# Message pass of a graph network kernel: totals loaded ahead of the masks, caps taken by DVE from the totals, the gate product on GpSimd, row copies by ScalarE and DVE by turns, stores issued by SyncE

## The chip, the cores and the metric

The kernel runs on one core of a Trainium2 chip, as one launch. The metric is the device time in microseconds, the median of several runs. Five engines run their own instruction streams and meet through semaphores: PE (TensorE, matmul), DVE (VectorE), ACT (ScalarE), POOL (GpSimd) and SP (SyncE, which here only issues transfers).

## The reference

Four graph layers run one after the other on 6250 nodes and 200000 edges, sorted by target node, with 64 channels. The change is in the third, a gated convolution:

```python
total = jnp.concatenate([atom_fea[dst], atom_fea[src], edge_fea], axis=1)
total = _batchnorm(total @ fc_w.T + fc_b, bn1_w, bn1_b)      # 128 columns per edge
gate, core = jnp.split(total, 2, axis=1)
messages = jax.nn.sigmoid(gate) * jax.nn.softplus(core)      # 64 columns per edge
aggr = jax.ops.segment_sum(messages, dst, num_segments=N)
```

## The kernel before

The kernel goes through the edges in seven passes. Two of them belong to this layer: `STAT` computes the sums `total @ fc_w.T` before the batch norm, stores them in DRAM (`total_d`) and gathers their mean and variance; `MSG`, the pass that is changed, reads them back and makes the messages and their running sums.

In `MSG` the edges stand in 196 blocks (`NB`). A block holds 512 edges (`BLK`) of each of two halves of the edge list, with 64 channels of each half on the 128 partitions, so that it is a tile of 128 x 1024: 512 columns of gate sums and 512 of core sums. Blocks go in fours (`U`), one round of a hardware loop (`IT` = 49 rounds); `i` counts rounds and `u` the block in a round, and every buffer of the pass but the masks, `pm` and `res` (two of each) stands four times. Every engine has its own code, and all wait through `Ring` semaphores: `s_x.done(engine, p, i, u, back=k)` waits until the producer of `s_x` is done with the block that is `k` before `u`. The code of each engine is written out in order, and this sets the order of the work; nothing is scheduled.

One block passes through these steps:

- SP loads `total_d` into `totals` (`attr_load`, L404, 512 KB; the tile is part of `feat`) once block u - 4 has been scaled (`s_col`), and for every second block a small mask (`mask_load`, L455), for which it waits until the scan three blocks back is over (`s_res`).
- POOL applies the batch norm with two `tensor_scalar` of 512 columns (`affine`, L624), with a scale `bnsc` and a shift `bnbi` per partition, into `zbuf`. The scale and shift of the gate are negated in advance, so that exp of it is exp(-gate).
- DVE caps all 1024 columns at 80 into `ebuf` (`capped`, L1387).
- ACT takes exp and then ln(1 + x) of the 1024 columns (`logs`, L1094 and L1096), and from the gate half exp(-x), the sigmoid, into `zbuf` (`gate`, L1100).
- DVE takes the larger of core and logarithm, the softplus, into `msg` (`softplus`, L1392), multiplies it with the sigmoid (L1485) and runs the segmented running sum (`scan`, L1376), whose mask PE has spread into PSUM (`spread_mask`, L816).
- PE turns the sums back into rows of edges (`turn_back`, L791), ACT copies them out of PSUM into `obuf` (`rows_out`, L1071) and issues their store (L1077, 256 KB) from its own queue, behind a wait for its copy.

The tiles `zbuf` and `ebuf` are parts of `arena`, `msg` and `res` are parts of `work`, `pm` and `pt` of `pn`. In its step for block k DVE does the softplus of k + 1, the cap of k + 2 and the scan of k; ACT does the gate of k + 1, the logs of k + 2 and the rows of k - 1.

Of the kernel before, what the change touches and what calls it, by code (L numbers as in the profile page):

```python
# [18 lines left out]
P = 128  # L19
# [3 lines left out]
J = 4  # L23
# [69 lines left out]
def gnn_kernel(nc, x, src, dst, ea128, ea16, ea64, W0, b0, W1, b1, W2, b2, fcw, fcb, bn1w, bn1b,  # L93
# [15 lines left out]
    with ctx:  # L109
# [80 lines left out]
        bnsc, bnbi = sb("bnsc", [P, 2]), sb("bnbi", [P, 2])  # L190
# [42 lines left out]
        s_col = ring("s_col", {**one(GATHER), MSG: 2})  # L233
# [99 lines left out]
        def _(sp):  # L333
# [66 lines left out]
            def attr_load(p, i, u):  # L400
                b = blk(i, u)
                if p == MSG:
                    s_col.done(sp, p, i, u, back=U)
                    sp.dma_start(totals[:, u, :], total_d[bass.ds(b, 1), :, :].rearrange("a p n -> (a p) n")).then_inc(s_att.sems[u], 16)  # L404
                if p not in (SOFT, STAT, *PNA):
                    return
                if p == SOFT:
                    s_col.done(sp, p, i, u, back=2)
                else:
                    s_eT.done(sp, p, i, u, back=U if p in PNA else 2)  # L410
                if p != MSG:
                    sp.sem_inc(s_in_order, 1)
                for h, e0 in ((0, 0), (1, BASE1)):
                    rows = bass.ds(b * BLK + e0, BLK)
                    if p == SOFT:
                        to = attr[:, u % 2, 0:2 * J * F].rearrange("p (j h c) -> p j h c", j=J, h=2)[:, :, h, :]
                        of = ea64[rows, :].rearrange("(p j) c -> p j c", j=J)
                    elif p == STAT:
                        to = attr[:, u % 2, h * J * P:(h + 1) * J * P]
                        of = ea128[rows, :].rearrange("(p j) c -> p (j c)", j=J)  # L420
                    elif p in PNA:
                        to = attr_to[u][:, h * F:h * F + F]
                        of = ea16[rows, :].rearrange("(p j) c -> p (j c)", j=J)
                    sp.dma_start(to, of).then_inc(s_att.sems[u], 16)
# [17 lines left out]
            def mask_load(p, i, u):  # L442
# [14 lines left out]
                for h in range(2):  # L457
                    sp.dma_start(keep[h * F:h * F + F, u // 2, :],
                                 keep_d[h:h + 1, bass.ds(blk(i, u) * BLK, 2 * BLK)].broadcast_to([F, 2 * BLK]))\
                      .then_inc(s_kee.sems[u], 16)  # L460

# [41 lines left out]
            for p in range(7):  # L503
# [15 lines left out]
                if p not in GCN:  # L519
# [25 lines left out]

                if p in READS:
# [27 lines left out]
        def _(g):  # L574
# [44 lines left out]
            def affine(i, u):  # L619
# [23 lines left out]
            for p in range(7):  # L643
# [4 lines left out]
                if p == MSG:  # L648
                    g.wait_ge(s_wc, 3)
                    for u in range(U):  # L650
                        affine(0, u)
                    with g.Fori(1, IT) as i:
                        for u in range(U):
                            affine(i, u)
                else:
# [36 lines left out]
        def _(pe):  # L692
# [82 lines left out]
            def turn_back(p, i, u):  # L775
# [11 lines left out]
                s_rev.done(pe, p, i, u, back=1)  # L787
                for k in range(UNITS[p]):
                    of = top[:, u, :] if p == SOFT and k == 0 else res[:, u % 2, k, :]
                    for j in range(J):  # L790
                        last = nc.tensor.transpose(pt[:, k, j * P:(j + 1) * P], of[:, 1 + j:1 + BLK:J], ident[:, :])  # L791
# [255 lines left out]
        def _(act):  # L1047
# [12 lines left out]

            def rows_out(p, i, u):
# [4 lines left out]
                to = rows_to[u] if K == 3 else obuf_f[:, u * BLK:(u + 1) * BLK]  # L1066
# [9 lines left out]
                r = runs3_d if K == 3 else runs1_d  # L1076
                act.dma_start(r.rearrange("(h n) c -> h n c", h=2)[:, bass.ds(blk(i, u) * BLK, BLK), :]  # L1077
# [33 lines left out]
            def body(p, i, end):  # L1111
                for u in range(U):
# [20 lines left out]
                    if p == MSG:  # L1133
# [82 lines left out]
            for p in range(7):  # L1216
# [23 lines left out]
                if p == MSG:  # L1240
                    rows_out(p, IT - 1, U - 1)
# [38 lines left out]
        def _(dve):  # L1280
# [103 lines left out]
            def capped(i, u):  # L1384

                s_col.done(dve, MSG, i, u)
                TS(ebuf[:, u, :], zbuf[:, u, :], CAP, None, ALU.min).then_inc(s_arg.sems[u], 1)  # L1387

            def softplus(i, u):
# [43 lines left out]
            def step(p, i, u, end):  # L1433
# [60 lines left out]
            def edge_pass(p):  # L1494
# [18 lines left out]
                for u in range(U):  # L1513
                    step(p, IT - 1, u, True)

# [360 lines left out]
            link(TS(bnbi[:, 0:1], bnbi[:, 0:1], -1.0, None, ALU.mult))  # L1876
            dve.sem_inc(s_wc, 1)
# [111 lines left out]
```

## Time and profile before

| | us |
|---|---|
| median of 3 runs | 10983.7 (10974.28 to 10992.69) |
| the profiled execution | 10998.39 |
| its span | 10996.7 |
| `MSG` within it, first cap to last row copy | 5731.3 to 6561.8 |

Outside `MSG` nothing is touched. Most of the time of the kernel is in the passes that gather node rows by indirect transfers on POOL; POOL is busy 64% of the span, PE 58%, DVE 52% and ACT 29%. `MSG` is the stretch of 830 us in slices 21 to 23 of the page's 40, in which ACT and DVE are busiest. The columns of the views are told with the rows below.

### The profile page before, as it was taken

The page shows a single profiled execution, that of the slowest core. Times are in us where ns is not written, and L with a number is a line of the kernel's source. Part 1 is how long each engine was busy: PE and PEld are TensorE (multiplying, and loading weights), DVE is VectorE, ACT ScalarE, POOL GpSimd, SP SyncE. Part 2 cuts the span into 40 slices and gives each one's busy share as a digit, 9 for nine tenths or more (in the row PEclk, how much of TensorE's full clock was granted, in tenths as well). Part 3 has the DMA queues.
Part 4 walks back from the last instruction along what each step waited for, and adds up shares of the span by engine and source line. Part 5 has one row for each costly group of instructions (what it writes and reads, how often), then busy time and mean ns, then how long its engine had stood idle before and what let it go on. Part 6 is the DMA issues. An engine that isn't in the chain of part 4 may idle for free. (4 is left out here: it accounts for less than half of the span.)

```text
span 10996.7 us, 138229 instructions
## 1 busy us (share of the span) xinstructions
PE 6379.7 (58%) x42657; PEld 5452.4 (50%) x42755; DVE 5713.8 (52%) x8038; ACT 3161.8 (29%) x4908; POOL 6995.6 (64%) x6971
## 2 busy tenths in 40 slices
PE   3666666548888566666653333455555455555553
PEld 2555555437788555445431113454544445555453
DVE  3555555689951655555557764333333443333335
ACT  1333333227710011111117761222222222222221
POOL 4777777715500577777764444777777767777774
PEclk9888888769999888888875556777777777777776
DMA  7666666514457477777765542444444334444442
GB/s 126 188 195 192 195 190 193 162 67 183 194 193 279 149 234 235 237 239 233 235 198 187 187 162 66 126 122 126 124 126 122 103 102 124 124 124 124 126 122 72
DMA packets 1299105, 1783.39 MB, mean 162 GB/s; under 512 B 619145, under 2 KB 794044, under 8 KB 1289322
## 3 DMA queue, kind: packets, MB, share of 16 engines
q1 hardware_dynamic: 816519, 882.68, 24.9%
q10 hardware_dynamic: 269696, 616.64, 15.2%
q0 software_dynamic: 212704, 281.43, 11.4%
q8 instruction: 136, 2.23, 0.1%
q14 instruction: 50, 0.41, 0.0%
HBM read 922.11 MB, written 857.87 MB: 162 GB/s over the span
## 5 line engine op out<-in xcount | busy, mean ns | idle before, releaser
L615 POOL DMA_INDIRECT arena<-table_d,idx_src x3136 | 2963.6, 945 | 1121.5 <-issue 955.3
L759 PE MATMUL pn<-work,wblk 128*128 128x128 f32 x3136 | 959.3, 405 | 1887.7 <-DMA arena<-table_d,idx_src 1887.7
L615 POOL DMA_INDIRECT arena<-in_x_dram,idx_src x1568 | 1523.7, 972 | 591.4 <-issue 477.0
L615 POOL DMA_INDIRECT arena<-tsrc_d,idx_src x1568 | 1482.1, 945 | 478.0 <-issue 478.0
L1329 DVE TENSOR_SCALAR idx_src<-src_all 128x8 int32 (+1 forms) x784 | 139.5, 179 | 3124.0 <-PE pn L760 2392.9
L759 PEld LDWEIGHTS pn<-work,wblk 128*128 128x128 f32 x3136 | 755.2, 296 | 1963.5 <-DMA arena<-table_d,idx_src 1005.9
L760 PE MATMUL pn<-ident,arena 128*128 128x128 f32 x4704 | 1292.6, 371 | 0.0
L1071 ACT ACTIVATE arena<-pn 128x512 f32<-128x512 f32 x1470 | 793.0, 594 | 1274.1 <-PE pn L791 1167.1
L760 PEld LDWEIGHTS pn<-ident,arena 128*128 128x128 f32 x4704 | 1096.6, 286 | 0.0
L749 PE MATMUL pn<-work,weT 128*128 128x512 f32 x784 | 553.9, 796 | 663.7 <-DMA arena<-tsrc_d,idx_src 635.8
L1376 DVE TENSOR_TENSOR_SCAN work<-keep,work,pn 128x512 f32<-128x512 bf16 x588 | 752.7, 1280 | 274.4 <-PE ph L772 203.0
L757 PE MATMUL pn<-ident,attr 128*128 128x128 f32 x1568 | 422.6, 362 | 627.8 <-DMA arena<-in_x_dram,idx_src 621.6
L791 PE MATMUL pn<-ident,work 128*128 128x128 f32 x2352 | 440.5, 334 | 510.7 <-ACT obuf L1071 499.6
L1087 ACT ACTIVATE work<-pe_ 128x1024 f32<-128x1024 f32 x196 | 200.9, 1025 | 1785.9 <-PE pe_ L730 1785.9
L757 PEld LDWEIGHTS pn<-ident,attr 128*128 128x128 f32 x1568 | 327.5, 258 | 741.3 <-issue 613.1
L624 POOL TENSOR_SCALAR arena<-feat,bnsc,bnbi 128x512 f32<-128x512 f32 x392 | 373.9, 966 | 486.7 <-DMA feat<-total_d 486.7
L791 PEld LDWEIGHTS pn<-ident,work 128*128 128x128 f32 x2352 | 351.0, 213 | 607.2 <-issue 315.7
L751 PEld LDWEIGHTS pn<-ident,arena 128*128 128x128 f32 x3136 | 509.5, 230 | 265.9 <-issue 265.9
L784 PE MATMUL pn<-ident,work 128*128 128x128 f32 x3528 | 582.6, 314 | 3.8 <-DVE work L1376 3.8
L640 POOL DMA_INDIRECT arena<-near_d,dlo x37 | 356.3, 9630 | 330.5 <-PE pe_ L900 276.2
L784 PEld LDWEIGHTS pn<-ident,work 128*128 128x128 f32 x3528 | 553.5, 215 | 4.2 <-DVE work L1376 4.2
L1179 ACT ACTIVATE feat<-pn 128x784 bf16<-128x784 f32 x592 | 487.2, 825 | 153.9 <-PE pn L911 144.6
(364 smaller groups left out, 13511.0 us busy)
## 6 DMA issues: line engine op xcount, KB each, us to landing
runs_d<-arena ACTq DMA_DIRECT2D x588, 768.0 KB
adj_d<-feat SPq DMA_DIRECT2D x37, 3136.0 KB, 10.7
feat<-adj_d SPq DMA_DIRECT2D x37, 3136.0 KB, 10.9
seed_d<-nothing SPq DMA_DIRECT2D x392, 256.0 KB
arena<-seed_d SPq DMA_DIRECT2D x392, 256.0 KB, 6.8
attr<-in_edge_attr_dram SPq DMA_DIRECT2D x392, 256.0 KB
feat<-total_d SPq DMA_DIRECT2D x196, 512.0 KB
keep<-keep_d SPq DMA_DIRECT2D x588, 128.0 KB
```

Source lines behind the costliest of these rows:

```text
L615: g.indirect_dma_start(out=to, out_offset=None, in_=table, in_offset=bass.IndirectOffsetOnAxis(ap=idx, axis=0))\
L624: g.tensor_scalar(zbuf[:, u, part * BLK:(part + 1) * BLK], totals[:, u, part * BLK:(part + 1) * BLK], bnsc[:, part:part + 1], bnbi[:, part ...
L749: mm(to, weT[:, :], eT[:, s, h * BLK:(h + 1) * BLK], start=True, stop=False, skip_group_check=True)
L751: last = mm(to[:, j:BLK:J], gat[:, u, j, h, :], ident[:, :], start=False, stop=True, skip_group_check=True)
L757: mm(to, attr[:, u % 2, j * P:(j + 1) * P], ident[:, :], start=True, stop=False, skip_group_check=True)
L759: mm(to, wblk[:, PNA.index(p), j, :], feat_to[u], start=True, stop=False, skip_group_check=True)
L760: last = mm(to, gat1[:, u, j * P:(j + 1) * P], ident[:, :], start=(p in (GCN1, GCN2)), stop=True, skip_group_check=True)
L784: last = nc.tensor.transpose(row_bank(u, k)[:, j * P:(j + 1) * P], res[:, u % 2, k, 1 + j:1 + BLK:J], ident[:, :])
L791: last = nc.tensor.transpose(pt[:, k, j * P:(j + 1) * P], of[:, 1 + j:1 + BLK:J], ident[:, :])
L1071: last = A(to.rearrange("p (h j k c) -> p k j h c", h=2, j=J, k=K)[:, k, :, :, :], of.rearrange("p (j h c) -> p j h c", j=J, h=2), ACT.Copy)
L1179: A(adj[:, m % 2, :, g * GROUP:(g + 1) * GROUP].rearrange("p k (b n) -> p k b n", b=2), pn[:, 2 * (k % 2):2 * (k % 2) + 2, 0:4 * KC].rearr ...
L1376: return SCAN(res[:, s, k, 1:BLK + 1], mask, data, res[:, 1 - s, k, BLK:BLK + 1], ALU.mult if mul else ALU.add, ALU.add if mul else ALU.mi ...
```

## The change

- SP issues the loads of two blocks ahead of their mask, where the mask came between them (`attr_load` of u and u + 1, then `mask_load` of u). A load now also waits for the cap of block u - 4 (`s_arg`), since DVE reads `totals` too.
- The cap no longer goes through POOL's `zbuf`. DVE computes min(total x scale, 80 - shift) for each half, two instructions of 512 columns, where `room` = 80 - shift is made once, and ACT adds the shift inside exp, which becomes two instructions of 512 columns with a bias per partition.
- POOL scales only the core half (one instruction a block) and takes over the product of softplus and sigmoid (`gated`), which stands in its queue behind the scaling of the next block.
- The row copy is ACT's for blocks 0 and 2 of a round and DVE's for blocks 1 and 3 (`gated_rows` on either). PE turns rows into two PSUM banks by turns where one was used.
- The stores of the pass are issued by SP (`gated_store`): block 0 of the round before behind the loads and the mask of blocks 0 and 1, blocks 1 to 3 of it behind those of 2 and 3.

```diff
@@ SP: attr_load @@
                     s_col.done(sp, p, i, u, back=U)
+                    sp.sem_inc(s_in_order, 1)
+                    s_arg.done(sp, p, i, u, back=U)
...
+            def gated_store(i, u):
+                s_rev.done(sp, MSG, i, u)
+                sp.sem_inc(s_in_order, 1)
+                sp.dma_start(runs1_d...[:, bass.ds(blk(i, u) * BLK, BLK), :]..., obuf_f[:, u * BLK:(u + 1) * BLK]...)
...
                             if p == MSG:
-                                attr_load(p, i, u)
-                                mask_load(p, i, u)
+                                if u % 2 == 0:
+                                    attr_load(p, i, u)
+                                    attr_load(p, i, u + 1)
+                                    mask_load(p, i, u)
+                                for v in ((0,), (), (1, 2, 3), ())[u]:
+                                    gated_store(i - 1, v)
@@ POOL: affine @@
-                for part in range(2):
-                    g.tensor_scalar(zbuf[:, u, part * BLK:(part + 1) * BLK], totals[:, u, part * BLK:(part + 1) * BLK],
-                                    bnsc[:, part:part + 1], bnbi[:, part:part + 1], ALU.mult, ALU.add).then_inc(s_col.sems[u], 1)
+                g.tensor_scalar(zbuf[:, u, BLK:], totals[:, u, BLK:], bnsc[:, 1:2], bnbi[:, 1:2], ALU.mult, ALU.add)\
+                 .then_inc(s_col.sems[u], 1)
+            def gated(i, u):
+                s_sg.done(g, MSG, i, u)
+                s_top.done(g, MSG, i, u)
+                g.sem_inc(s_go, 1)
+                g.tensor_tensor(msg[:, u, :], msg[:, u, :], zbuf[:, u, 0:BLK], ALU.mult).then_inc(s_cus.sems[u], 1)
...
                         for u in range(U):
                             affine(i, u)
+                            gated(i - 1 if u == 0 else i, (u - 1) % U)
@@ PE: turn_back @@
-                s_rev.done(pe, p, i, u, back=1)
+                s_rev.done(pe, p, i, u, back=2 if p == MSG else 1)
@@ ACT: gated_rows, logs, body @@
+                A(obuf_f[:, u * BLK:(u + 1) * BLK]..., pt[:, u % 2, :]..., ACT.Copy).then_inc(s_rev.sems[u], 1)
...
-                A(ebuf[:, u, :], ebuf[:, u, :], ACT.Exp).then_inc(s_exp.sems[u], 1)
+                A(ebuf[:, u, 0:BLK], ebuf[:, u, 0:BLK], ACT.Exp, bias=bnbi[:, 0:1])
+                A(ebuf[:, u, BLK:], ebuf[:, u, BLK:], ACT.Exp, bias=bnbi[:, 1:2]).then_inc(s_exp.sems[u], 1)
...
-                        if u > 0:
-                            rows_out(p, i, u - 1)
-                        elif not (isinstance(i, int) and i == 0):
-                            rows_out(p, i - 1, U - 1)
+                        if u % 2:
+                            gated_rows(i, u - 1)
@@ DVE: capped, gated_rows, softplus, step @@
-                s_col.done(dve, MSG, i, u)
-                TS(ebuf[:, u, :], zbuf[:, u, :], CAP, None, ALU.min).then_inc(s_arg.sems[u], 1)
+                s_att.done(dve, MSG, i, u)
+                s_sg.done(dve, MSG, i, u, back=U)
+                s_top.done(dve, MSG, i, u, back=U)
+                TS(ebuf[:, u, 0:BLK], totals[:, u, 0:BLK], bnsc[:, 0:1], room[:, 0:1], ALU.mult, ALU.min)
+                TS(ebuf[:, u, BLK:], totals[:, u, BLK:], bnsc[:, 1:2], room[:, 1:2], ALU.mult, ALU.min).then_inc(s_arg.sems[u], 1)
+                V.tensor_copy(obuf_f[:, u * BLK:(u + 1) * BLK]..., pt[:, u % 2, :]...).then_inc(s_rev.sems[u], 1)
...
+                s_col.done(dve, MSG, i, u)
                 s_ln.done(dve, MSG, i, u)
+                s_res.done(dve, MSG, i, u, back=U)
                 TT(msg[:, u, :], zbuf[:, u, BLK:], ebuf[:, u, BLK:], ALU.max).then_inc(s_top.sems[u], 1)
...
-                    s_sg.done(dve, p, i, u)
-                    s_top.done(dve, p, i, u)
-                    TT(msg[:, u, :], msg[:, u, :], zbuf[:, u, 0:BLK], ALU.mult).then_inc(s_cus.sems[u], 1)
...
+                    if u == 2:
+                        gated_rows(i, 1)
+                    if u == 0 and not (isinstance(i, int) and i == 0):
+                        gated_rows(i - 1, U - 1)
@@ DVE: before the pass @@
+            link(TS(room[:, :], bnbi[:, :], -1.0, CAP, ALU.mult, ALU.add))
```

DVE's queue in the hardware loop, blocks 0 and 1 of a round, before. L1485 is the product, L1392 the softplus of the next block, L1387 the cap of the one after, L1376 the scan:

```order
L1485 TENSOR_TENSOR work<-work,arena 128x512
L1392 TENSOR_TENSOR work<-arena 128x512
L78 ISA
L1387 TENSOR_SCALAR arena<-arena 128x1024
L78 REGISTER_ALU
L1376 SCALAR_TENSOR_TENSOR work<-pn,work 128x512
L1485 TENSOR_TENSOR work<-work,arena 128x512
L1392 TENSOR_TENSOR work<-arena 128x512
L1387 TENSOR_SCALAR arena<-arena 128x1024
L1376 SCALAR_TENSOR_TENSOR work<-pn,work 128x512
```

The same place now, with the lines of the changed file: L1435 is the softplus, L1420 and L1421 the cap, L1427 the row copy, L1407 the scan:

```order
L1435 TENSOR_TENSOR work<-arena 128x512
L78 ISA
L1420 TENSOR_SCALAR arena<-feat,bnsc,room 128x512
L1421 TENSOR_SCALAR arena<-feat,bnsc,room 128x512
L78 ISA
L1427 COPY obuf<-pn 128x4x2x64
L78 REGISTER_ALU
L1407 SCALAR_TENSOR_TENSOR work<-pn,work 128x512
L1435 TENSOR_TENSOR work<-arena 128x512
L1420 TENSOR_SCALAR arena<-feat,bnsc,room 128x512
L1421 TENSOR_SCALAR arena<-feat,bnsc,room 128x512
L1407 SCALAR_TENSOR_TENSOR work<-pn,work 128x512
```

The product has left DVE's queue, the cap is two instructions on `feat` (the totals) with scalars per partition, and a copy stands ahead of the scan in every second step.

ACT's queue in the loop, two steps before. L1100 is the gate, L1094 and L1096 exp and ln, L1071 the row copy, L1077 its store:

```order
L1100 ACTIVATE arena<-arena 128x512
L1094 ACTIVATE arena<-arena 128x1024
L1096 ACTIVATE arena<-arena 128x1024
L78 ISA
L1071 ACTIVATE obuf<-pn 128x4x2x64
L1077 ISA
L1077 DMA runs_d<-obuf 128x2x256
```

Two steps of it now, with L1135 the gate, L1128 and L1129 exp, L1131 ln and L1093 the row copy:

```order
L1135 ACTIVATE arena<-arena 128x512
L78 REGISTER_ALU
L1128 ACTIVATE arena<-arena,bnbi 128x512
L1129 ACTIVATE arena<-arena,bnbi 128x512
L1131 ACTIVATE arena<-arena 128x1024
L1135 ACTIVATE arena<-arena 128x512
L1128 ACTIVATE arena<-arena,bnbi 128x512
L1129 ACTIVATE arena<-arena,bnbi 128x512
L1131 ACTIVATE arena<-arena 128x1024
L78 ISA
L1093 ACTIVATE obuf<-pn 128x4x2x64
```

The store has left the queue, and the copy stands in every second step.

## Rows read from the trace of the kernel before

**Rows 1.** The page: span and instruction count.

```profile
span 10996.7 us, 138229 instructions
```

**Rows 2.** Groups by form, 5725 to 6575 us: count | busy us, mean ns | idle before, releaser.

```profile
L624 POOL TENSOR_SCALAR arena<-feat,bnsc,bnbi 128x512 f32<-128x512 f32 x392 | 373.9, 966 | 486.7 <-DMA feat<-total_d 486.7
L1376 DVE TENSOR_TENSOR_SCAN work<-pn,work 128x512 f32<-128x512 f32 x196 | 249.8, 1274 | 0.0
L1096 ACT ACTIVATE arena<-arena 128x1024 f32<-128x1024 f32 x196 | 207.1, 1057 | 6.2
...
L1392 DVE TENSOR_TENSOR work<-arena 128x512 f32<-128x512 f32 x196 | 149.7, 764 | 73.3 <-ACT arena L1096 67.1
L1485 DVE TENSOR_TENSOR work<-work,arena 128x512 f32<-128x512 f32 x196 | 142.9, 729 | 23.4 <-DVE work L1376 9.9
...
L1387 DVE TENSOR_SCALAR arena<-arena 128x1024 f32<-128x1024 f32 x196 | 135.5, 691 | 84.9 <-POOL arena L624 84.9
L1100 ACT ACTIVATE arena<-arena 128x512 f32<-128x512 f32 x196 | 123.5, 630 | 136.5 <-ACT obuf L1071 136.4
```

**Rows 3.** Line L1094 (exp): ns min/median/max, first and last start, its waits.

```profile
L1094 ACT ACTIVATE arena<-arena x196: 1038/1056/1057, 5732.0 to 6553.5; 128x1024 f32<-128x1024 f32 x196
its engine sat idle before it (us, times) until:
  DVE arena L1387: 88.0, 87
```

**Rows 4.** Timeline, 6000 to 6018: start, duration, engine, line [idle before, releaser].

```profile
6001.83 0.69 DVE L1392 TENSOR_TENSOR work<-arena 128x512 f32<-128x512 f32 x1 [0.48 <-ACT arena L1096]
6001.95 4.00 POOL L624 TENSOR_SCALAR arena<-feat,bnsc,bnbi 128x512 f32<-128x512 f32 x4 [4.57 <-DMA feat<-total_d]
...
6003.95 0.69 DVE L1387 TENSOR_SCALAR arena<-arena 128x1024 f32<-128x1024 f32 x1 [1.43 <-POOL arena L624]
...
6004.68 1.06 ACT L1094 ACTIVATE arena<-arena 128x1024 f32<-128x1024 f32 x1 [1.10 <-DVE arena L1387]
...
6006.45 1.20 SPq L404 DMA_DIRECT2D feat<-total_d  x2
...
6008.28 0.63 ACT L1100 ACTIVATE arena<-arena 128x512 f32<-128x512 f32 x1 [0.97 <-ACT obuf L1071]
...
6008.82 1.04 ACT L1094 ACTIVATE arena<-arena 128x1024 f32<-128x1024 f32 x1
...
6009.89 1.06 ACT L1096 ACTIVATE arena<-arena 128x1024 f32<-128x1024 f32 x1
6010.01 1.52 POOL L624 TENSOR_SCALAR arena<-feat,bnsc,bnbi 128x512 f32<-128x512 f32 x2 [4.06 <-DMA feat<-total_d]
6010.85 0.58 ACT L1071 ACTIVATE obuf<-pn 128x512 f32<-128x512 f32 x1
6010.98 1.10 DVE L1392 TENSOR_TENSOR work<-arena 128x512 f32<-128x512 f32 x1 [0.85 <-ACT arena L1096]
...
6012.00 0.68 DVE L1387 TENSOR_SCALAR arena<-arena 128x1024 f32<-128x1024 f32 x1
6012.05 0.63 ACT L1100 ACTIVATE arena<-arena 128x512 f32<-128x512 f32 x1 [0.61 <-ACT obuf L1071]
...
6012.71 1.06 ACT L1094 ACTIVATE arena<-arena 128x1024 f32<-128x1024 f32 x1
```

**Rows 5.** The transfer queues, 5725 to 6575 us: packets, MB, share of 16 engines.

```profile
q1 hardware_dynamic: 28760, 103.21, 36.7%
q10 hardware_dynamic: 53312, 51.39, 17.2%
```

**Rows 6.** Single lines: ns min/median/max; two with a scalar per partition (L1523, L1828).

```profile
L1523 DVE TENSOR_SCALAR arena<-arena,valid x6: 254/254/254, 6636.3 to 10937.0; 128x64 f32<-128x64 f32 x6
L1567 DVE TENSOR_SCALAR nrow<-nrow x3: 195/195/195, 6649.9 to 10942.3; 128x64 f32<-128x64 f32 x3
L1828 DVE TENSOR_SCALAR arena<-dlo x698: 278/286/289, 3059.9 to 3629.4; 128x128 f32<-128x128 f32 x175
L1755 DVE COPY feat<-pn x13: 279/682/692, 3660.4 to 3702.5; 128x512 f32<-128x512 f32 x12, 128x128 f32<-128x128 f32 x1
L624 POOL TENSOR_SCALAR arena<-feat,bnsc,bnbi x392: 766/773/1717, 5729.7 to 6551.5; 128x512 f32<-128x512 f32 x196
```

**Rows 7.** Timeline, 5737.1 to 5738.3 us, DVE and POOL at once.

```profile
5736.91 0.69 DVE L1392 TENSOR_TENSOR work<-arena 128x512 f32<-128x512 f32 x1 [0.49 <-ACT arena L1096]
5737.05 1.72 POOL L624 TENSOR_SCALAR arena<-feat,bnsc,bnbi 128x512 f32<-128x512 f32 x1
5737.53 0.68 DVE L1387 TENSOR_SCALAR arena<-arena 128x1024 f32<-128x1024 f32 x1
5738.13 1.27 DVE L1376 TENSOR_TENSOR_SCAN work<-pn,work 128x512 f32<-128x512 f32 x1
```

More of the change, by code:

```diff
@@ L189, in gnn_kernel @@
         agg2 = sb("agg2", [P, 2])
-        bnsc, bnbi = sb("bnsc", [P, 2]), sb("bnbi", [P, 2])
+        bnsc, bnbi, room = sb("bnsc", [P, 2]), sb("bnbi", [P, 2]), sb("room", [P, 2])
         nrow = sb("nrow", [P, 4, F])
@@ L232, in gnn_kernel @@
         s_eC = ring("s_eC", one((STAT, *PNA)))
-        s_col = ring("s_col", {**one(GATHER), MSG: 2})
+        s_col = ring("s_col", {**one(GATHER), MSG: 1})
         s_zero_out = sem("s_zero_out")
@@ L460, in mask_load @@
                       .then_inc(s_kee.sems[u], 16)
+            def gated_store(i, u):
+                s_rev.done(sp, MSG, i, u)
+                sp.sem_inc(s_in_order, 1)
+                sp.dma_start(runs1_d.rearrange("(h n) c -> h n c", h=2)[:, bass.ds(blk(i, u) * BLK, BLK), :]
+                             .rearrange("h (p j) c -> p h (j c)", j=J),
+                             obuf_f[:, u * BLK:(u + 1) * BLK].rearrange("p (h q) -> p h q", h=2)).then_inc(s_out.sems[u], 16)
             def adjacency_moves(p):
@@ L544, in _ @@
                     continue
+                if p == MSG:
+                    for u in range(U):
+                        gated_store(IT - 1, u)
                 if p in READS:
@@ L651, in _ @@
                         affine(0, u)
+                    for u in range(U - 1):
+                        gated(0, u)
                     with g.Fori(1, IT) as i:
@@ L654, in _ @@
                             affine(i, u)
+                            gated(i - 1 if u == 0 else i, (u - 1) % U)
+                    gated(IT - 1, U - 1)
                 else:
@@ L790, in turn_back @@
                     for j in range(J):
-                        last = nc.tensor.transpose(pt[:, k, j * P:(j + 1) * P], of[:, 1 + j:1 + BLK:J], ident[:, :])
+                        last = nc.tensor.transpose(pt[:, u % 2 if p == MSG else k, j * P:(j + 1) * P], of[:, 1 + j:1 + BLK:J], ident[:, :])
                 last.then_inc(s_row.sems[u], 1)
@@ L1059, in masks, with gated_rows @@
                 A(neg[:, v, :], keep[:, v, :], ACT.Copy, scale=BIG, bias=-BIG).then_inc(s_neg.sems[u], 1)
+            def gated_rows(i, u):
+                s_row.done(act, MSG, i, u)
+                s_out.done(act, MSG, i, u, back=U)
+                A(obuf_f[:, u * BLK:(u + 1) * BLK].rearrange("p (h j c) -> p j h c", h=2, j=J),
+                  pt[:, u % 2, :].rearrange("p (j h c) -> p j h c", j=J, h=2), ACT.Copy).then_inc(s_rev.sems[u], 1)
             def rows_out(p, i, u):
@@ L1065, in rows_out @@
                 K = UNITS[p]
-                to = rows_to[u] if K == 3 else obuf_f[:, u * BLK:(u + 1) * BLK]
+                to = rows_to[u]
                 for k in range(K):
@@ L1075, in rows_out @@
                 s_rev.done(act, p, i, u)
-                r = runs3_d if K == 3 else runs1_d
-                act.dma_start(r.rearrange("(h n) c -> h n c", h=2)[:, bass.ds(blk(i, u) * BLK, BLK), :]
+                act.dma_start(runs3_d.rearrange("(h n) c -> h n c", h=2)[:, bass.ds(blk(i, u) * BLK, BLK), :]
                               .rearrange("h (p j) c -> p h (j c)", j=J),
@@ L1239, in _ @@
                 body(p, IT - 1, True)
-                if p == MSG:
-                    rows_out(p, IT - 1, U - 1)
                 if p == SOFT:
@@ L1384, in capped, with gated_rows, softplus @@
             def capped(i, u):
+                s_att.done(dve, MSG, i, u)
[3 more added lines that the diff above has]
+                TS(ebuf[:, u, BLK:], totals[:, u, BLK:], bnsc[:, 1:2], room[:, 1:2], ALU.mult, ALU.min).then_inc(s_arg.sems[u], 1)
+            def gated_rows(i, u):
+                s_row.done(dve, MSG, i, u)
+                s_out.done(dve, MSG, i, u, back=U)
+                V.tensor_copy(obuf_f[:, u * BLK:(u + 1) * BLK].rearrange("p (h j c) -> p j h c", h=2, j=J),
+                              pt[:, u % 2, :].rearrange("p (j h c) -> p j h c", j=J, h=2)).then_inc(s_rev.sems[u], 1)
+            def softplus(i, u):
                 s_col.done(dve, MSG, i, u)
-                TS(ebuf[:, u, :], zbuf[:, u, :], CAP, None, ALU.min).then_inc(s_arg.sems[u], 1)
-            def softplus(i, u):
                 s_ln.done(dve, MSG, i, u)
+                s_res.done(dve, MSG, i, u, back=U)
                 TT(msg[:, u, :], zbuf[:, u, BLK:], ebuf[:, u, BLK:], ALU.max).then_inc(s_top.sems[u], 1)
@@ L1514, in edge_pass @@
                     step(p, IT - 1, u, True)
+                if p == MSG:
+                    gated_rows(IT - 1, U - 1)
             over_f = lambda a: a.unsqueeze(2).broadcast_to([P, a.shape[1], F])
```

## The prediction

> **What bounds the kernel now.** The change touches only `MSG`, so I first read the groups of its stretch [rows 2]. Every engine has idle time: POOL is busy 374 of some 830 us, the three DVE instruction kinds and the scan sum to 678, ACT's groups shown to 536 with the row copies to come. No engine is full, so the time is set by a circle of waits or by arrivals. The pace is one block in (6553.5 - 5732.0) / 195 = 4.21 us [rows 3].
>
> The timeline shows the circle [rows 4]. ln of a block begins at 6009.89 and ends at 6010.95; the softplus starts 0.03 later; the cap of the next block follows at 6012.00 and ends at 6012.68; exp starts at 6012.71. Then exp and ln again. Softplus (block k + 1), cap (k + 2), exp and ln (k + 2), softplus (k + 2): each waits for the one before, whatever the engines have free. With the softplus at its usual pitch of 0.61 (0.69 less the 0.08 by which back-to-back DVE instructions overlap), the circle is 0.03 + 0.61 + 0.69 + 0.03 + 1.04 + 0.03 + 1.06 = 3.49 us.
>
> Three things lift it to 4.21. First, ACT has a circle of its own: from one exp to the next in these rows exp takes 1.07 to the start of ln, 0.96 until the row copy starts, 1.20 until the gate starts (the copy, a wait for it and the issue of its store), and 0.54 from gate to exp [rows 4]: 3.77 us. The page has 136.5 us of idle time before the gate behind the copy, 0.70 a block [rows 2]. Second, loads come late: at 6001.83 the softplus is done in good time, but POOL gets its block only at 6001.95, the cap waits 1.43 us for it and exp another 1.10 behind [rows 4]. The cap waited 84.9 us for POOL, exp 88.0 for the cap, of which 27.1 lie before the first block: 61, or 0.31 a block [rows 2, 3]. Third, DVE and POOL get in each other's way: the softplus takes 0.764 on average against 0.69 undisturbed, POOL's scaling 0.966 against 0.773 [rows 2, 6], and the softplus of 1.10 us started while POOL was in its second instruction [rows 4]. 3.77 plus 0.31 plus 0.1 or so is the 4.2 seen.
>
> **The change, part by part.** I work out the new circle and then look whether anything else is longer.
>
> *ACT.* Exp becomes two instructions of 512. One of 512 lasts 0.63 [rows 2], and a next one that waits for nothing starts 0.54 after it (gate at 8.28, exp at 8.82) [rows 4]. So 0.54 + 0.63 = 1.17 in place of 1.04: +0.13. ln stays 1.06, and waits 0.03 for exp. ACT's own circle loses the store and the wait for the copy, and every second copy: gate 0.54, exp 0.54 + 0.66, ln 1.06, half a copy 0.25, in all 3.05 us. It stops being a bound; between the end of ln and the next exp it has at most copy and gate, 1.0 us, beside the 1.5 that DVE needs there.
>
> *DVE, the cap.* Two instructions of 512 with scalars per partition. One with such a scalar takes 254 ns for 64 columns, against 195 without: +59 ns; from 64 to 128 columns it adds 32 ns, the same 0.5 ns a column as without [rows 6]. So the cap's pace per column (1024 in 691 ns) is kept: 0.286 + 384 x 0.52 ns = 0.486 us for 512 [rows 2, 6]. Its pitch is 0.06 less, 0.42, by the overlap of DVE's neighbours. The pair lasts 0.42 + 0.49 = 0.91 in place of 0.69: +0.22. No row has two such scalars; another 59 ns on each would make it 1.03, and a half of the old cap each 0.76. I take 0.91.
>
> *DVE, waits.* The softplus now stands behind the scan and five waits. Those on blocks long finished come after the one on ln, so I take 0.10 from ln to the softplus in place of 0.03.
>
> *New circle:* 0.10 + 0.61 + 0.91 + 0.04 + 1.17 + 0.03 + 1.06 = 3.92 us. With the low ends of lag and cap 3.70, with the high cap 4.04.
>
> *DVE's load.* Softplus 0.61, cap 0.84, scan 1.2, and in every second step a copy out of PSUM, 0.68 by the copy of the same size in L1755, pitch 0.6 [rows 6]: 3.3 us in such a step, plus 0.35 for waits that can only be passed when the scan is over. 3.7 is just under 3.92, so the copy is covered by DVE's wait for ln; if the cover goes, a step with a copy costs what is over.
>
> *The product on POOL.* It needs softplus and sigmoid, and the scan needs it a whole step later, some 4 us, so its duration is hidden unless it is over 3 us. No row shows POOL with two inputs; the nearest is its scaling at 0.77 [rows 6], which bounds it from below, and twice that, 1.54, from above. POOL is then busy 0.8 + 0.8 to 1.5 of 3.9 us. I take 1.2. The Trainium skill (GPSIMD Engine Reference, "Elementwise — side-by-side cycle accounting") gives 4497 ns for an addition of 2048 columns on GpSimd, 1.96 times DVE's; a quarter is 1.1 us, an estimate from that page which no row here shows.
>
> *Loads.* The cap of block u needed POOL's scaling, two instructions; now it needs only the load, 1.5 us earlier. In the order of SP's queue the loads of blocks 0 and 1 stand behind the last store of the round before, which waits for DVE's row copy at 2.3 us into the step of block 0, four blocks ahead; the cap that needs it comes two steps and 0.7 us after that step began, 8.5. One load takes from its issue at 6006.45 to POOL at 6010.01 3.56 us, with a store beside it [rows 4]; a store occupies the 16 engines for 0.172 x 850 / 196 = 0.75 us and a load for 1.6 [rows 5]. Load behind a store: 2.6 + 3.6 + 0.8 = 7.0, 1.5 us early. Loads of 2 and 3 have more. So the 0.31 a block goes. All of it now stands in one queue, which has to be busy 2.35 of 3.92 us.
>
> *Ends of the pass.* The first cap comes 1.6 us earlier (two scalings of POOL), `room` costs 0.2. PE's second bank takes nothing off the circle: PE waits in it anyway.
>
> **The sum.** 195 x (4.21 - 3.92) = 57, plus 1.4, say 58 us less. The profiled execution lasts 10998.4 (span 10996.7 [rows 1]), 14.7 over the median of 10983.7, so I give the change against either: 10940 profiled, median 10926. Range of the mechanism itself: 3.70 gives -100, 4.04 gives -35.
>
> **Rivals.**
>
> *Loads stay late* (a queue with stores ahead of loads). For it: SP now waits for ACT and DVE copies before it may load, and any lag of these is passed on. Against: the 1.5 us reckoned above. Price: the 0.31 of before comes back on top of 3.92: 4.23, time as before, 10983, "no change".
>
> *POOL's product blocks the cap* (the slower side). The product becomes ready when softplus and sigmoid are, that is while DVE starts the first half of the cap. If POOL gets to memory between the two halves, the second waits for the whole product, and the circle with it: 1.2 - 0.15 = 1.05 us. In every second step (after odd blocks ACT copies first, so the product comes too late to hurt) that gives 3.92 + 0.52 = 4.44: +45, 11029; in every step 4.97: +148, 11132. It decides from 0.3 us a block on. For it: DVE instructions are held when POOL is in one, softplus 1.10 in place of 0.69 [rows 4]. Against: at 5737.05 a scaling of POOL was pending, DVE went from softplus to cap without a gap, and POOL lasted 1.72, until 0.56 after the cap's end [rows 7]; so it is DVE's neighbour that gets in first. One case, but the one wanted. Besides, POOL has two waits and a semaphore to pass before the product.
> The Trainium skill (SBUF — State Buffer, "Who interferes with whom") says that DVE instructions with two inputs in SBUF or in the two-port mode, and those of GpSimd, take the shared port for their whole duration, and the other blocks fully. The trace agrees: 1.10 and 1.72 are about a whole instruction of the other more, less 0.15 to 0.3. Its rule speaks against this change, which gives POOL an instruction of two inputs and DVE two short ones in place of one.
>
> *DVE becomes the bound.* If copies and waits make 4.1 in the steps with a copy, the mean is 4.0: -40, 10943; it lies in the range.
>
> **How the numbers follow.** The circle at 3.92, with DVE's share in it: 0.78. Loads late: 0.10. POOL blocks the cap: 0.12, a third of it so mild (under 0.3 us a block) that the result is no slower. What can be told from no change here is 0.2%, 22 us. Faster: 0.78 and a few of each rival, 0.82. Same: 0.09. Slower: 0.09. Range: from 3.75 (-90) to the lower end of the rivals, 10980.
>
> **What would show it.** Exp first to last start over 195 at 3.85 to 4.0 us; no wait of the cap for a load; the gate no longer behind a row copy for 136 us; cap halves near 0.49; the softplus waiting for ln in every step; POOL's product 0.8 to 1.5. Wrong if the cap's second half averages over 0.8 (blocked by POOL), if DVE waits for `total_d`, or if the scan waits for POOL.

## The result

| | before, us | this kernel, us | ratio, 95% interval |
|---|---|---|---|
| changed kernel | 10982.83 | 11116.45 (11108.69 to 11139.15) | 1.0128 (1.0113 to 1.0143) |

Slower by 134 us, where 58 less was forecast; the time lies 136 us over the upper end of the range. It is the second rival (GpSimd's product blocks DVE's cap, 11029 to 11132), which had 0.12. The prediction's own sign for it, a second half of the cap over 0.8 us on average, is there: 1.26.

The groups of the message pass in the profile after, 5700 to 6720 us; they answer to [rows 2]. L1420 and L1421 are the two halves of the cap, L1128 and L1129 exp, L1131 ln, L1135 the gate, L1435 the softplus, L649 the product:

```profile
L649 POOL TENSOR_TENSOR work<-work,arena 128x512 f32<-128x512 f32 x196 | 273.8, 1397 | 492.4 <-ACT arena L1135 274.7 <-DVE work L1435 217.7
L1407 DVE TENSOR_TENSOR_SCAN work<-pn,work 128x512 f32<-128x512 f32 x196 | 249.2, 1271 | 0.1
L1421 DVE TENSOR_SCALAR arena<-feat,bnsc,room 128x512 f32<-128x512 f32 x196 | 246.0, 1255 | 0.0
...
L641 POOL TENSOR_SCALAR arena<-feat,bnsc,bnbi 128x512 f32<-128x512 f32 x196 | 168.0, 857 | 71.7 <-DMA feat<-total_d 71.6
...
L1128 ACT ACTIVATE arena<-arena,bnbi 128x512 f32<-128x512 f32 x196 | 141.4, 722 | 349.5 <-DVE arena L1421 349.5
L1129 ACT ACTIVATE arena<-arena,bnbi 128x512 f32<-128x512 f32 x196 | 138.3, 706 | 0.0
...
L1420 DVE TENSOR_SCALAR arena<-feat,bnsc,room 128x512 f32<-128x512 f32 x196 | 106.0, 541 | 4.2 <-DMA feat<-total_d 4.2
```

The two halves of the cap are the same instruction on different columns, yet the first takes 0.54 us and the second 1.26 on average. The single line of each shows the first and last start of exp, which give the pace as in [rows 3]:

```profile
L1128 ACT ACTIVATE arena<-arena,bnbi x196: 706/722/724, 5717.9 to 6675.4; 128x512 f32<-128x512 f32 x196
L1421 DVE TENSOR_SCALAR arena<-feat,bnsc,room x196: 538/1485/1515, 5717.4 to 6673.8; 128x512 f32<-128x512 f32 x196
```

(6675.4 - 5717.9) / 195 = 4.91 us a block, 0.70 more than before; times 195 that is 136 us, the whole of the loss. The timeline of one step, with its releasers, answers to [rows 4]:

```profile
6200.25 0.63 ACT L1135 ACTIVATE arena<-arena 128x512 f32<-128x512 f32 x1
6200.45 0.69 DVE L1435 TENSOR_TENSOR work<-arena 128x512 f32<-128x512 f32 x1 [0.89 <-ACT arena L1131]
...
6201.06 0.54 DVE L1420 TENSOR_SCALAR arena<-feat,bnsc,room 128x512 f32<-128x512 f32 x1
6201.31 1.41 POOL L649 TENSOR_TENSOR work<-work,arena 128x512 f32<-128x512 f32 x1 [1.67 <-DVE work L1435]
6201.51 1.49 DVE L1421 TENSOR_SCALAR arena<-feat,bnsc,room 128x512 f32<-128x512 f32 x1
6202.92 1.27 DVE L1407 TENSOR_TENSOR_SCAN work<-pn,work 128x512 f32<-128x512 f32 x1
6203.03 0.72 ACT L1128 ACTIVATE arena<-arena,bnbi 128x512 f32<-128x512 f32 x1 [2.15 <-DVE arena L1421]
...
6214.70 1.06 ACT L1131 ACTIVATE arena<-arena 128x1024 f32<-128x1024 f32 x1
...
6215.79 0.69 DVE L1435 TENSOR_TENSOR work<-arena 128x512 f32<-128x512 f32 x1 [1.30 <-ACT arena L1131]
...
6216.85 0.54 DVE L1421 TENSOR_SCALAR arena<-feat,bnsc,room 128x512 f32<-128x512 f32 x1
6216.97 1.55 POOL L649 TENSOR_TENSOR work<-work,arena 128x512 f32<-128x512 f32 x1 [3.03 <-ACT arena L1135]
```

The softplus ends at 6201.14; 0.17 later the product is ready, while the first half of the cap runs. The product goes next, the second half waits for it, and exp behind it. In the last two rows, where ScalarE's row copy made the gate late, the product becomes ready 0.12 after the second half began: that half lasts 0.54, and the product waits. In the other step with a row copy the softplus and the cap are 0.2 late too, and the product still comes 0.03 ahead of the second half. Of the 196 second halves 147 last over 1 us and 49 do not: the first two blocks, and one step of the round in 47 rounds.

### The profile page after: what moved, and what is told of

It is laid out like the page before. It is cut to its first block, busy times and chain, and to the rows that moved or that the text cites. A ratio compares the mean times of both kernels' runs of the same rounds, so it can differ in the third digit from the quotient of the medians.

```text
span 11112.7 us, 139561 instructions
## 1 busy us (share of the span) xinstructions
PE 6432.9 (58%) x42755; PEld 5482.6 (49%) x42755; DVE 5808.1 (52%) x8137; ACT 3165.2 (28%) x5006; POOL 7063.8 (64%) x6971
## 4 chain that ended last, share of the span: by engine, by line
POOL 53%; issue 20%; DVE 11%; PE 5%; ACT 5%; DMA 4%; SPq 1%; POOLq 0%; DVEq 0%; ACTq 0%
POOL arena L633 52%; DVE obuf L1853 2%; DVE arena L1421 2%; ACT arena L1131 2%; DMA feat<-adj_d 2%; POOL feat L714 2%; PE pn L968 1%; PE pn L955 1%; ACT arena L1128 1%; DMA arena<-near_d,dlo 1%; ACT arena L1129 1%; DVE neg L1853 1%; DVE pos L1853 1%; DVE arena L1420 1%; PE ph L955 1%
## 5 line engine op out<-in xcount | busy, mean ns | idle before, releaser
L1407 DVE TENSOR_TENSOR_SCAN work<-keep,work,pn 128x512 f32<-128x512 bf16 x588 | 752.8, 1280 | 276.1 <-PE ph L800 205.8
L1121 ACT ACTIVATE work<-pe_ 128x1024 f32<-128x1024 f32 x196 | 200.7, 1024 | 1783.3 <-PE pe_ L758 1783.3
L649 POOL TENSOR_TENSOR work<-work,arena 128x512 f32<-128x512 f32 x196 | 273.8, 1397 | 492.4 <-ACT arena L1135 274.7
```

The source lines that it names most:

```text
L1407: return SCAN(res[:, s, k, 1:BLK + 1], mask, data, res[:, 1 - s, k, BLK:BLK + 1], ALU.mult if mul else ALU.add, ALU.add if mul else ALU.mi ...
```

## The experiments

"Pace" is exp's first to last start over 195, from the profile of each run; before it is 4.21, after 4.91. Ratios are to the kernel before on the same chip. The third column is the difference of the medians, and the ratio is not exactly their quotient: for `c_load_order` the one gives 58 us and the other 68. `h_half_product`, `u_first_half_two_inputs`, `x_one_input_scalars` and `y_one_input_constants` leave out part of the arithmetic and serve for timing alone. On two of the chips the kernel before takes 13279 and 13380 us, since the other passes take longer (`c_load_order` reaches its first exp at 7279 us in place of 5732); in the message pass, undisturbed instructions last the same on all, so the pace is compared across them and times are not.

| run | pace, us | this - before, us | ratio, 95% interval |
|---|---|---|---|
| `a_product_after_cap` | 4.19 | +17 | 1.0011 (0.9977 to 1.0045) |
| `b_product_on_dve` | 4.18 | +9 | 1.0006 (0.9980 to 1.0031) |
| `h_half_product` | 4.50 | +68 | 1.0037 (1.0007 to 1.0067) |
| `c_load_order` | 3.88 | -58 | 0.9949 (0.9922 to 0.9975) |
| `d_rows_and_stores` | 3.99 | -49 | 0.9955 (0.9938 to 0.9971) |
| `w_rows_third_store_act` | 3.77 | -89 | 0.9940 (0.9921 to 0.9958) |
| `m_cap_first` | 4.11 | -22 | 0.9981 (0.9972 to 0.9991) |
| `n_cap_first_pool_product` | 4.33 | +18 | 1.0016 (1.0006 to 1.0026) |
| `o_after_cap_first` | 3.54 | -141 | 0.9872 (0.9856 to 0.9889) |
| `v_cap_first_third_store_act` | 3.47 | -140 | 0.9904 (0.9881 to 0.9928) |
| `u_first_half_two_inputs` | 5.28 | +168 | 1.0130 (1.0096 to 1.0165) |
| `x_one_input_scalars` | 4.19 | -12 | 0.9988 (0.9977 to 0.9999) |
| `y_one_input_constants` | 4.42 | +28 | 1.0029 (1.0016 to 1.0041) |
| `r_split_exp` | 4.26 | -11 | 1.0001 (0.9983 to 1.0019) |

**Is it the product between the halves?** Three edits of the changed kernel.

```diff
+                s_arg.done(g, MSG, i + (u + 1) // U, (u + 1) % U)     # in gated: wait for the next cap
```

> The changed kernel, but GpSimd's product of block k waits also until DVE has capped block k + 1 (the last block excepted). Theory (the product takes the shared way to memory between the two halves of the cap): the second half falls from 1.49 to 0.54 us in every block, and the pace from 4.91 to the 4.15 that the changed kernel's undisturbed steps show, so 195 x 0.76 = 148 us less than the changed kernel: 10968. Rival (the exp with a bias per partition, the two short instructions or the stores on SyncE's queue cost the time, and the long second half is only where the waiting shows): the pace stays over 4.6 us, 11055 or more.

Measured: the second half at 0.535/0.541/0.544 us, the pace 4.19. The theory holds; the rival (4.6 and more) falls.

```diff
+                    TT(msg[:, u, :], msg[:, u, :], zbuf[:, u, 0:BLK], ALU.mult).then_inc(s_cus.sems[u], 1)   # DVE
-                            gated(i - 1 if u == 0 else i, (u - 1) % U)                                      # POOL
```

> The changed kernel, but DVE does the product, ahead of the softplus, as before; GpSimd has only the scaling of the core half. Theory (blocked cap): the second half lasts 0.54; DVE then has 0.61 + 0.61 + 0.99 + 1.20 + half of 0.60 = 3.7 us a block and 0.35 of waits behind the scan, so the pace is 4.15 to 4.25 us: 10972 to 10991. Rival (exp and stores cost the time): 4.8 to 5 us, 11100 or more.

Measured: pace 4.18, as expected; second half 0.54 in the median. In 28 blocks it lasts 0.83 or more: there GpSimd's scaling of the core half gets in between the halves, of which more below.

```diff
-                g.tensor_tensor(msg[:, u, :], msg[:, u, :], zbuf[:, u, 0:BLK], ALU.mult)...
+                g.tensor_tensor(msg[:, u, 0:BLK // 2], msg[:, u, 0:BLK // 2], zbuf[:, u, 0:BLK // 2], ALU.mult)...
```

> The changed kernel, with GpSimd's product on 256 of its 512 columns only (the rest of the messages stays the softplus without the gate). Theory (the cap's second half waits for the whole of the product): it falls from 1.49 by what the product gets shorter, about 0.6, to 0.9 us, and the pace from 4.91 to about 4.5: 11036. Rival (a collision has a fixed price whatever the length): the second half stays near 1.49 and the time at 11116.

The second half of the cap (L1421) and the product (L649) in this run:

```profile
L1421 DVE TENSOR_SCALAR arena<-feat,bnsc,room x196: 539/946/976, 7302.9 to 8180.5; 128x512 f32<-128x512 f32 x196
L649 POOL TENSOR_TENSOR work<-work,arena x196: 722/850/1012, 7308.3 to 8185.1; 128x256 f32<-128x256 f32 x196
```

The product got shorter by 0.54 (median 1.387 to 0.850), and so did the second half (1.485 to 0.946). The wait follows the length of GpSimd's instruction one to one; the pace of 4.50 is the one expected.

**What the other parts bring.** The load order alone, in the kernel before:

```diff
-                                attr_load(p, i, u)
-                                mask_load(p, i, u)
+                                if u % 2 == 0:
+                                    attr_load(p, i, u)
+                                    attr_load(p, i, u + 1)
+                                    mask_load(p, i, u)
```

> The kernel before, with the loads of two blocks issued ahead of their mask and nothing else. Theory (the loads were late because they stood behind a mask that waits for a scan): the cap's waits for GpSimd behind a load go (0.31 us a block) and the pace falls from 4.21 to 3.9: 10923. Rival (the loads are late because the transfers are slow, or the circle of ScalarE takes over at once): 4.1 to 4.2 us, 10960 to 10983.

The cap waited 5.9 us in all for GpSimd, where [rows 2] has 84.9; pace 3.88. The theory holds. The load order alone brings the 58 us that the prediction gave the whole change (66 by the pace).

`d_rows_and_stores` adds the stores by SyncE, the copies by turns and the two banks, and keeps scaling, cap and product as before:

> The kernel before with the parts of the change that move no arithmetic: loads ahead of masks, stores by SyncE, row copies by ScalarE and DVE by turns, two PSUM banks for the rows. Scaling of both halves (GpSimd), one cap of 1024 columns and the product (DVE) as before. Theory (these parts are the gain, the cap in halves and the product on GpSimd are the loss): circle 0.10 + 0.61 + 0.69 + 0.04 + 1.05 + 0.03 + 1.06 = 3.58 us, DVE's load 3 x 0.61 + 1.20 + 0.30 + 0.35 = 3.7; pace 3.7, the pass 722 us in place of 821, 100 us less than before. Rival (the load order alone is the gain, the rest nothing, as DVE gets the copies): 3.87 as with the load order alone, 60 to 65 us less than before.

Both miss: 3.99 is slower than the load order alone. The timeline shows SyncE, GpSimd and the cap (L1412):

```profile
6007.59 3.14 SPq L467 DMA_DIRECT2D runs_d<-obuf  x3
...
6011.42 1.00 SPq L405 DMA_DIRECT2D feat<-total_d  x2
...
6015.62 3.23 POOL L640 TENSOR_SCALAR arena<-feat,bnsc,bnbi 128x512 f32<-128x512 f32 x3 [5.65 <-DMA feat<-total_d]
...
6017.60 0.69 DVE L1412 TENSOR_SCALAR arena<-arena 128x1024 f32<-128x1024 f32 x1 [1.43 <-POOL arena L640]
```

The loads are issued behind three stores that take 3.1 us to get out, since the third waits for DVE's copy, and the cap then waits for them. Moving only that store to ScalarE:

```diff
-                                for v in ((0,), (), (1, 2, 3), ())[u]:
+                                for v in ((0,), (), (1, 2), ())[u]:
+                        if u == 1 and not (isinstance(i, int) and i == 0):     # ScalarE
+                            gated_store(i - 1, U - 1)
```

> d_rows_and_stores, but the store of block 3 of a round is issued by ScalarE instead of SyncE, so that no load stands behind a wait for DVE's row copy. Theory (in d_rows_and_stores every fourth step lasts 4.66 us in place of 3.77 because the next loads stand behind that store): the long step shrinks by the 1.5 to 2 us that the loads are issued earlier, as far as it was caused by them: pace 3.78 to 3.85 in place of 3.99. Rival (the loads are late because all stores share their queue and go first): 3.95 to 4.0 as before.

3.77: the long step of 4.66 is 3.76. The theory holds, and most of the 100 us that `d_rows_and_stores` should have shown is there (89) once this wait is out of the queue of loads.

**Breaking the circle.** In DVE's step the cap of block k + 2 goes ahead of the softplus of k + 1:

```diff
-                        softplus(i + (u + 1) // U, (u + 1) % U)
-                        capped(i + (u + 2) // U, (u + 2) % U)
+                        capped(i + (u + 2) // U, (u + 2) % U)
+                        softplus(i + (u + 1) // U, (u + 1) % U)
```

> As d_rows_and_stores, and DVE caps block k + 2 before it takes the softplus of block k + 1. Theory (the circle softplus, cap, exp, ln sets the pace): the cap no longer waits for ln, the circle is gone, DVE's load of 3.4 to 3.6 us is the bound: 3.5, 140 us less than before. Rival (DVE was full already): 3.7 as without, 100 less.

> As m_cap_first, with the product on GpSimd (which scales both halves too). Theory (shared way to memory: GpSimd 0.77 + 0.77 + 1.27 less some 0.2 each, DVE 0.69 for the cap and 0.69 for the softplus, one at a time): 3.4 to 3.6 us, no better than m_cap_first. Rival (each engine's own load counts): ScalarE's 3.0 to 3.1 us is the bound, 220 us less than before.

> The changed kernel with one thing other: DVE caps block k + 2 before the softplus of block k + 1. The product needs that softplus, so it can't come between the halves of the cap, and ln is no longer in the circle. Theory: the second half lasts 0.54, ScalarE's load 1.34 + 0.03 + 1.06 + 0.54 + 0.25 = 3.2 us is the bound, with what collisions add 3.3 to 3.4: 160 to 175 us less than before. Rival (another cost of the change, as the exp with bias or the stores on one queue, holds the pace): 4.1 us or more as with the product behind the cap.

The first two miss. `m_cap_first` is slower than `d_rows_and_stores`: it has the same late loads (GpSimd waits 403.8 us for them) and needs them earlier by one softplus; that this is all of the 0.12 us was not tested. In `n_cap_first_pool_product` GpSimd's queue makes a new circle, here softplus (L1429), product (L648), two scalings and the cap (L1416):

```profile
6201.02 0.68 DVE L1429 TENSOR_TENSOR work<-arena 128x512 f32<-128x512 f32 x1
...
6201.89 1.27 POOL L648 TENSOR_TENSOR work<-work,arena 128x512 f32<-128x512 f32 x1 [1.61 <-DVE work L1429]
...
6203.14 1.52 POOL L640 TENSOR_SCALAR arena<-feat,bnsc,bnbi 128x512 f32<-128x512 f32 x2
6204.69 0.69 DVE L1416 TENSOR_SCALAR arena<-arena 128x1024 f32<-128x1024 f32 x1 [1.79 <-POOL arena L640]
6205.30 0.69 DVE L1429 TENSOR_TENSOR work<-arena 128x512 f32<-128x512 f32 x1
```

4.28 us from softplus to softplus, each released by the one before or next behind it in its queue. In `o_after_cap_first` the cap needs no scaling, so this circle is not there: pace 3.54, 141 us less than before and 275 less than the changed kernel (134 more and 141 less than before). It beats both, and its rival of 4.1 us falls; but its theory promised 3.3 to 3.4 us and 160 to 175 less, with a second half of 0.54 throughout. In 48 of 196 blocks that half lasts 0.83 or more, since GpSimd's scaling gets in:

```profile
6103.57 0.55 DVE L1420 TENSOR_SCALAR arena<-feat,bnsc,room 128x512 f32<-128x512 f32 x1 [0.23 <-DVE work L1407]
6103.59 1.01 POOL L641 TENSOR_SCALAR arena<-feat,bnsc,bnbi 128x512 f32<-128x512 f32 x1
...
6104.04 0.84 DVE L1421 TENSOR_SCALAR arena<-feat,bnsc,room 128x512 f32<-128x512 f32 x1
```

That is 0.07 us a block of DVE's time (whether all of it reaches the pace was not tested), and late loads are another 0.07 of the pace, as the next run shows; the rest of the shortfall is open.

`v_cap_first_third_store_act` is that kernel with the edit of the third store:

> o_after_cap_first with the same edit of the third store. Theory: its step of 3.89 falls to 3.5, the pace from 3.54 to 3.45: 18 us less than o_after_cap_first, 155 to 160 less than the kernel before. Rival (the loads share a queue with the stores): the same as o_after_cap_first, 141 less.

Pace 3.47, its step of 3.89 is 3.52. The profile bears the step out, and 14 of the 18 us between the two. The 155 to 160 us less than before are not reached: 140 by the times, 145 by the pace. The times of this run and of `o_after_cap_first`, on different chips, cannot rank the two.

**Why the product gets in, when a scaling in [rows 7] did not.** The first half of the cap as an instruction with two inputs:

```diff
-                TS(ebuf[:, u, 0:BLK], totals[:, u, 0:BLK], bnsc[:, 0:1], room[:, 0:1], ALU.mult, ALU.min)
+                TT(ebuf[:, u, 0:BLK], totals[:, u, 0:BLK], totals[:, u, BLK:], ALU.min)
```

> The changed kernel with the first half of the cap replaced by the smaller of gate and core sums, an instruction with two inputs from memory (0.69 us in place of 0.54; the gate is then not what the reference wants). The question is why GpSimd got in between the two halves here, where a scaling that waited while DVE went from softplus to cap in the kernel before did not. Theory A (a two-input instruction hands on to the next one of DVE, an instruction in the two-port mode does not): the second half lasts 0.54 in most blocks, the product 1.8 to 2.0, and the pace is 4.2 to 4.4 us: about 11010. Theory B (GpSimd gets in whenever it waits at the end of a DVE instruction): the second half lasts 1.3 to 1.5, the pace is 4.9 to 5.1: 11120 or more.

Second half 1.486 in the median, long in 194 of 196 blocks: Theory A falls, since the product gets in behind a DVE instruction of either kind. The pace of 5.28 is over the 4.9 to 5.1 of Theory B, by the longer first half (0.14) and the blocks that are now hit as well. Then GpSimd's, with one input in the product's place:

```diff
-                g.tensor_tensor(msg[:, u, :], msg[:, u, :], zbuf[:, u, 0:BLK], ALU.mult)...
+                g.tensor_scalar(msg[:, u, :], msg[:, u, :], bnsc[:, 1:2], bnbi[:, 1:2], ALU.mult, ALU.add)...   # x
+                g.tensor_scalar(msg[:, u, :], msg[:, u, :], 0.5, 0.25, ALU.mult, ALU.add)...                    # y
```

> The changed kernel with GpSimd's product replaced by a scaling of the softplus, one input and two scalars per partition, in the same place and behind the same waits (the gate is left out of the message). Theory (it is the two-input instruction that gets in): the second half lasts 0.54 in every block, the replacement 1.1 to 1.4 where it waits for it, and the pace is 4.1 to 4.2 us, 0 to 20 us less than the kernel before. Rival (any GpSimd instruction that becomes ready in the first half gets in): the second half lasts about 1.0, the pace is 4.5 us, 55 us more.

> As x_one_input_scalars, with constants in place of the scalars per partition (the gate is left out of the message). Theory (number of inputs): as there, second half 0.54, pace 4.1 to 4.2 us. Rival (a scaling comes late to memory only because it fetches its scalars first): the second half lasts about 1.0 and the pace is 4.5 us.

The second half of the cap in x, and then in y, each with GpSimd's instruction:

```profile
L1421 DVE TENSOR_SCALAR arena<-feat,bnsc,room x196: 537/541/546, 5720.7 to 6537.9; 128x512 f32<-128x512 f32 x196
L649 POOL TENSOR_SCALAR work<-work,bnsc,bnbi x196: 768/1122/1193, 5726.3 to 6542.2; 128x512 f32<-128x512 f32 x196
```

```profile
L1421 DVE TENSOR_SCALAR arena<-feat,bnsc,room x196: 539/839/874, 5724.1 to 6586.3; 128x512 f32<-128x512 f32 x196
L649 POOL TENSOR_SCALAR work<-work x196: 617/738/898, 5729.6 to 6590.8; 128x512 f32<-128x512 f32 x196
```

In x, with scalars per partition, it waits until DVE's second half is over and never delays the cap; in y, with constants and also one input, it gets in between and costs the cap 0.3 us. So my theory of the number of inputs falls, and the rival of y holds in kind (it expected 1.0 and 4.5; measured 0.84 and 4.42): the scalars make the difference.

They do not keep GpSimd out, though; they make it need a longer lead. Over all runs I took the places where a scaling with scalars per partition was pending as the first half of the cap gave way to the second. It got in 124 times, with leads of 0.38 to 1.01 us from its start to that of the second half (in `b_product_on_dve`, `o_after_cap_first` and `v_cap_first_third_store_act`), and 269 times it did not, with leads of 0.35 or less. In x the leads are 0.18 or less. A product or a scaling with constants needs no more than 0.03 and 0.02. From the softplus to a cap, the place of [rows 7] with its lead of 0.48, no scaling got in with a lead under 0.66; over that some did and some did not. What GpSimd does in that lead, and why DVE's instruction matters to a scaling and not to the product, is not shown.

**The price of exp.** In the kernel before, exp in two halves with no bias per partition:

> The kernel before with exp in two instructions of 512 columns and no bias per partition. In the changed kernel each of the two lasts 0.72 and 0.71 where the gate, of the same size, lasts 0.63. Theory (the bias per partition costs 0.09): 0.63 for both here, the pace as before or 0.1 more: 10983 to 11003. Rival (it is the place of the tile or the missing scale): 0.71 here too.

```profile
L1094 ACT ACTIVATE arena<-arena x196: 612/629/632, 7309.7 to 8140.9; 128x512 f32<-128x512 f32 x196
L1095 ACT ACTIVATE arena<-arena x196: 612/613/617, 7310.3 to 8141.5; 128x512 f32<-128x512 f32 x196
```

0.63 and 0.61, against 0.72 and 0.71 with the bias: the bias per partition costs 0.09 each. The time is the same as before within 0.2%, the pace 0.05 longer.

## Why the prediction was wrong

- *POOL blocks the cap.* This is the step that failed. The prediction had the mechanism and its place, gave it 0.12, and turned it down by one row: a scaling that let DVE pass [rows 7]. That row shows an instruction with scalars per partition and a lead of 0.48 us; the product has no such scalars, and `x_one_input_scalars` and `y_one_input_constants` show that without them an instruction gets in at the short leads of this place. The estimate that the product comes too late after odd blocks was wrong as well: it is late enough in one step of four. 147 of 196 blocks by 0.95 us are 0.71 us a block, and 4.19 (with the product held back) + 0.71 = 4.90. That the rival's upper case, 1.05 us in every step on top of 3.92, gives 4.97 beside the measured 4.91 is luck: its circle was 0.27 too short, and its price a block 0.34 too high.
- *The new circle at 3.92.* Mis-sized even without a collision: `a_product_after_cap` gives 4.19, no gain, so this step alone would have sunk the forecast of 58 us less. The pair of exp takes 0.63 + 0.71 = 1.34 in place of 1.17, since the bias was costed at nothing; the pair of the cap 0.45 + 0.54 = 0.99 in place of 0.91. Together 0.25 of the 0.27 missing. For exp a rule would have helped that the prediction did not look up: the Trainium skill (ScalarE: Activation LUTs, "What ACT_TABLE_LOAD costs") gives 0.09 us for each operand per partition, and `r_split_exp` agrees.
- *The product's duration*, 1.2, hidden: it is 1.27 free, and its duration was indeed not what hurt in the scan, which never waits for it; it hurt in the cap. Costing an instruction by who waits for its result left out who waits for the memory.
- *Loads.* Right for the changed kernel: the cap waits 4.2 us in all for them. The reason is that its cap reads the sums itself. In `d_rows_and_stores`, where a scaling stands between, the same queue order costs 0.22 us a block, the first rival in another kernel.
- *The softplus behind five waits*: 0.10 was taken from ln to the softplus. The ln before the softplus of 6215.79 is fast to follow (6214.70 + 1.06 = 6215.76, 0.03 later), the one before 6200.45 ends at 6200.22, 0.23 earlier. In `a_product_after_cap` two steps of a round take 4.09 to 4.10 and two 4.29, with lags of 0.03 and 0.23, so the mean lag is 0.13: the last 0.02 to 0.03 of the 0.27. Why two of the four are late is open.
- *DVE as the bound*: not seen. DVE waits 216 us for ln.
- *The Trainium skill's rule* on the shared port (SBUF — State Buffer, "Who interferes with whom"), cited against the change, was the better guide than the single row: `h_half_product` shows the cap waiting for the product, 0.54 less for 0.54 less. The section also says that the order of issue, and not the kind of instruction, decides who blocks whom. The product agrees (0.03 us ahead of the second half it goes first, 0.11 behind it does not); the scaling of `x_one_input_scalars` does not, if issue is its start in the profile, which is up to 0.18 ahead. The prediction read 1.10 and 1.72 as a whole instruction of the other engine more. They are less: 1.10 holds the last 0.55 of a scaling, less 0.14, and 1.72 the last 0.55 of the softplus and the cap's 0.61, less 0.21.

## What to carry to other kernels

Before a part of the work moves to GpSimd, look at what DVE runs at the moment the part becomes ready, and above all at chains of short DVE instructions on the path: a dependence that makes it ready just then costs nearly its full length, once a block. A wait that holds it back took the same change from 134 us more to the time of before (17 us more, within noise), and an order of DVE in which the critical instructions come before the one that releases it took it to 141 less. And evidence of who goes first holds only for the instruction, and for the lead, that it shows.

## What the runs showed of the hardware

- GpSimd and DVE, 128 x 512, f32: a GpSimd product or a scaling with constants that is ready during one half of the cap goes ahead of the next (1.49 and 0.84 in place of 0.54). The price is GpSimd's own length, less some 0.32: 1.27 gives 0.95, with 256 columns 0.72 gives 0.40, with constants 0.62 gives 0.30.
- A GpSimd scaling with two scalars per partition (0.77 alone) goes ahead of the second half if it has started 0.38 us or more before it (124 times, 0.84 in place of 0.54), and not at 0.35 or less (269 times). Then, in x, it ends 0.47 to 0.48 after that half, and 0.64 in the step with a row copy.
- A product ready 0.03 us before the second half starts still goes first; 0.11 after it does not.
- ScalarE's exp of 512 columns takes 0.71 to 0.72 with a bias per partition and 0.61 to 0.63 without.
- DVE's `tensor_scalar` of 512 columns with two scalars per partition takes 0.54, one of 1024 columns with a constant 0.69: half the columns take well over half the time.
